# Two graph layers on one core: the stretch between the layers and the opening of layer 1 rearranged

## What is computed

```python
h = jnp.maximum(_layernorm(x, axis=-1), 0.0)
x = x + _L0_gnn_ref(h, edge_index, L0_gnn_W, L0_gnn_b)      # h@W, normed by degree, summed over edges, + b; h + gelu(..)
h = jnp.maximum(_layernorm(x, axis=-1), 0.0)
# layer 1:
message_in = jnp.concatenate((source_x, target_x, edge_x), axis=1)
message_x = _mlp(message_in, msg_W1, msg_b1, msg_W2, msg_b2)
agg = jax.ops.segment_sum(message_x, targets, num_segments=num_nodes)
update_in = jnp.concatenate((agg, node_x), axis=1)
x = x + _mlp(update_in, upd_W1, upd_b1, upd_W2, upd_b2)
```

## Time and profile before

| | us |
|---|---|
| median of 3 runs | 2396.71 (2395.64 to 2399.2) |
| the profiled execution | 2395.71, its span 2393.9, mean TensorE clock 0.938 |
| busy: TensorE, its weight loads | 2169.2, 1951.6 |
| busy: VectorE, ScalarE, GpSimd | 1706.6, 1143.6, 1600.1 |
| layer 0's edges | about 197 to 804 us of the span |
| between the layers | about 804 to 889 |
| message passes of layer 1 | about 889 to 2354 |
| tail | about 2354 to 2393.9 |

### The profile page before, as it was taken

One profiled execution on the slowest core, in us unless ns is written; L12 is line 12 of the kernel. 1 busy time (PEld: TensorE's weight loads), 2 busy tenths in 40 slices (PEclk: granted clock), 3 DMA queues, 4 the chain that ended last, 5 costly groups with the idle time before them and its releaser, 6 DMA issues.

```text
span 2393.9 us, 72611 instructions
## 1 busy us (share of the span) xinstructions
PE 2169.2 (91%) x23690; PEld 1951.6 (82%) x23690; DVE 1706.6 (71%) x4619; ACT 1143.6 (48%) x2411; POOL 1600.1 (67%) x1574
## 2 busy tenths in 40 slices
PE   2255999999999569999999999999999999999998
PEld 1143888887888458999999999999999999999995
DVE  8866888887888766666666666666666666666662
ACT  0004888888888433444444444444444444444442
POOL 5375777777775115777777777777777777777771
PEclk7566999999999758999999999999999999999999
DMA  2002111111111022333333333333333333333332
GB/s 73 1 1 44 26 27 28 27 28 28 27 27 19 4 68 59 74 73 73 76 75 74 73 73 73 73 73 76 74 74 74 75 73 75 76 74 73 73 74 36
DMA packets 345718, 133.10 MB, mean 56 GB/s; under 512 B 304301, under 2 KB 321555, under 8 KB 345587
## 3 DMA queue, kind: packets, MB, share of 16 engines
q1 hardware_dynamic: 297780, 82.40, 15.2%
q0 software_dynamic: 47808, 49.05, 11.3%
HBM read 123.78 MB, written 7.52 MB: 55 GB/s over the span
## 4 chain that ended last, share of the span: by engine, by line
PE 87%; DVE 7%; issue 3%; POOL 2%; DMA 1%; ACT 1%; SPq 0%; DVEq 0%; PEld 0%; PEldq 0%; POOLq 0%; ACTq 0%
PE psum L1737 17%; PE psum L1679 14%; PE psum L1548 12%; PE psum L1751 12%; PE psum L1580 9%; PE psum L1670 8%; PE psum L1689 5%; PE psum L1569 2%; PE psum L1715 2%; POOL rows L665 1%; PE psum L1704 1%; PE psum L1559 1%; PE psum L1640 1%; PE psum L1515 1%; DVE work L813 1%
## 5 line engine op out<-in xcount | busy, mean ns | idle before, releaser
L665 POOL DMA_INDIRECT rows<-a_rows,idx x1078 | 1049.8, 974 | 449.9 <-issue 306.0
L1319 ACT ACTIVATE hT<-psum 128x392 bf16<-128x392 f32 x1152 | 510.7, 501 | 101.6 <-PE psum L1580 93.4
L665 POOL DMA_INDIRECT rows<-g_rows,idx x416 | 431.4, 1037 | 145.8 <-issue 126.7
L1548 PE MATMUL psum<-work,hT 128*128 128x192 bf16 x3528 | 455.5, 247 | 0.3 <-ACT hT L1319 0.3
L1737 PE MATMUL psum<-edge_index,H 128*128 128x192 bf16 x4802 | 429.9, 247 | 2.4 <-DVE H L1092 2.4
L1372 ACT ACTIVATE eoT<-psum 128x512 f32<-128x512 f32 x392 | 213.8, 602 | 409.3 <-PE psum L1670 409.3
L1737 PEld LDWEIGHTS psum<-edge_index,H 128*128 128x128 bf16 x4802 | 398.9, 99 | 4.0 <-DVE H L1092 2.5
L1548 PEld LDWEIGHTS psum<-work,hT 128*128 128x128 bf16 x3528 | 324.0, 99 | 71.0 <-issue 1.4
L1580 PE MATMUL psum<-Z,one_lo 128*128 128x392 f16 x1152 | 365.5, 339 | 15.6 <-DVE Z L929 15.4
L1679 PE MATMUL psum<-wb,eoT 128*128 128x64 f32 x3136 | 376.0, 273 | 0.0
L1679 PEld LDWEIGHTS psum<-wb,eoT 128*128 128x128 f32 x3136 | 367.3, 193 | 0.1
(11 more groups left out here) (272 smaller groups left out, 2060.2 us busy)
## 6 DMA issues: line engine op xcount, KB each, us to landing
work<-in_edge_attr_dram SPq DMA_DIRECT2D x390, 128.0 KB
rows<-a_rows,idx POOLq DMA_INDIRECT x1078
Z<-slot_code SPq DMA_DIRECT2D x98, 160.0 KB
rows<-g_rows,idx POOLq DMA_INDIRECT x416
idx<-src_by_tile SPq DMA_DIRECT2D x199, 4.0 KB
wb<-b_rows SPq DMA_DIRECT2D x196, 16.0 KB, 2.0
g_rows<-Y SPq DMA_DIRECT2D x1, 1600.0 KB, 8.9
a_rows<-Y SPq DMA_DIRECT2D x6, 256.0 KB, 2.6
```

What stands on the lines that cost most here:

```text
L665: pool.indirect_dma_start(out=rows[:, k, t, :], out_offset=None, in_=table, in_offset=bass.IndirectOffsetOnAxis(ap=idx[:, k, t:t + 1], axis=0)
L1319: nc.scalar.activation(counts[:, j % 2, :, t * SLOTS:(t + 1) * SLOTS], psum[:, t % 4, 0:KEYS].rearrange("p (h m) -> p h m", m=SLOTS), ACT.Copy
L1548: ins = TT.matmul(psum[:, 4 + (j + 1) % 2, 0:NPART * D], counts[:, (j + 1) % 2, h, :], gtab[:, h, :, :].rearrange("p k d -> p (k d)"), sta ...
```

## The change

1. `centre`: the multiplication into `mean` goes; one scalar_tensor_tensor computes `Y = s1 * (-1/D) + X`.
2. The addition of `b_upd2` leaves GpSimd; VectorE does it after the message passes, ahead of the outputs. `s_xb` goes.
3. The setup between the layers goes. For the first pass `rel` is the one of layer 0 plus `pe_far`, added behind the last variance; `rnd_no`, `slot_cmp` and `pe_slot` are set by GpSimd before layer 0. (If layer 0 needed several passes, VectorE resets `rel` behind them.)
4. The opening of layer 1 on every engine: packing and spreading first, transposes of superblock 0 under them, picks, and only then the transposes of superblock 1 and the edge terms of superblock 0. TensorE's wait for `s_tab3` stands behind the packing.
5. SyncE: the features and indices of superblock 0 are loaded already during the interlude; in the loop they are loaded at the end of the turn before. Indices are issued ahead of the window load. The wait for `a_rows` is gone from SyncE; VectorE waits only for the first `C_USED` (4) chunks of it, since the passes overwrite only that part of `Y`; GpSimd waits for all. The load of the counts into `hT` moves from between the layers to the end of the passes.

```diff
+        C_USED = -(-(o + BINS * NPART * D // 2) // (T * D))
@@ SyncE
-            sp.wait_ge(s_hrow, 1)
-            sp.dma_start(hT[0:1, :], cnt_dram...).then_inc(s_cntr, 16)
...
-            def load_superblock(r, s, k, tiles, rest):
-                sp.wait_ge(summed[1], r * NSB + s + 1)
+            def load_inputs(s, k, tiles=T, rest=None):
                 if rest is None:
...
+                if k != KPE:
+                    sp.dma_start(idx[:, k, :], src_dram[:, bass.ds(s * T, T)]).then_inc(idx_in[1][k], 16)
+            def inputs_free(n, k):
+                sp.wait_ge(summed[1], n + 1)
+                if k != KPE:
+                    sp.wait_ge(added, n + 1)
+            def load_window(s, k):
                 b0 = sp.value_load(base_i[0:1, bass.ds(s, 1)], min_val=0, max_val=NP - W)
                 sp.dma_start(wb[D:2 * D, k, :], b_dram[bass.ds(b0, W), :]).then_inc(b_in[k], 16)
-                if k != KPE:
-                    sp.wait_ge(added, r * NSB + s + 1)
-                    sp.dma_start(idx[:, k, :], ...).then_inc(idx_in[1][k], 16)
+            def load_superblock(r, s, k, tiles, rest):
+                if k:
+                    inputs_free(r * NSB + s, k)
+                    load_inputs(s, k, tiles, rest)
+                load_window(s, k)
+            sp.wait_ge(s_stT, 1)
+            load_inputs(0, 0)
             for c in range(NCHUNK):
...
-            sp.wait_ge(s_ad, 16 * NCHUNK)
             sp.wait_ge(s_bd, 16 * NCHUNK)
...
+                sp.wait_ge(from_slot_ready, 2 * r * NIT + 1)
                 load_codes(r, 0, 0)
...
+                    inputs_free(r * NSB + (i + 1) * U, 0)
+                    load_inputs((i + 1) * U, 0)
...
+                inputs_free((r + 1) * NSB, 0)
+                load_inputs(0, 0)
+            sp.wait_ge(s_hrow, 1)
+            sp.dma_start(hT[0:1, :], cnt_dram...).then_inc(s_cntr, 16)
@@ GpSimd
+            nc.gpsimd.memset(rnd_no[:, :], 0.0)
+            nc.gpsimd.iota(slot_cmp[:, :], [[P, BINS]], base=-CENTRE, channel_multiplier=1, ...)
+            G.tensor_copy(pe_slot, rank32)
-            pool.wait_ge(s_var[1], NCHUNK)
-            nc.gpsimd.tensor_tensor(X[:, :, :], X[:, :, :], bu3, ALU.add).then_inc(s_xb, 1)
-            pool.wait_ge(s_ad, 16 * NCHUNK)
+            pool.wait_ge(s_ad[0], 16 * C_USED)
+            pool.wait_ge(s_ad[1], 16 * (NCHUNK - C_USED))
@@ VectorE
-                    dve.wait_ge(counts_reset[1], r + 1)
-                    dve.sem_inc(s_turn[2], 1)
-                    for k in range(3):
-                        onehots_of(0, k)
                     edges_to_slots(0, 0, first=True)
                     copy_packed(0, 0)
+                    onehots_of(0, 0)
                     edges_to_slots(0, 1, first=True)
                     picks(0, 0)
                     copy_packed(0, 1)
+                    for k in range(1, 3):
+                        onehots_of(0, k)
+                    dve.wait_ge(s_bd, 16 * NCHUNK)
                     slots_to_edges(0, 0)
...
-                link(V.tensor_scalar(mean[:, cols], s1[:, cols], 1.0 / D, None, ALU.mult))
-                V.tensor_tensor(Y[:, cols, :], X[:, cols, :], per_node(mean, c), ALU.subtract).then_inc(s_centred, 1)
+                V.scalar_tensor_tensor(Y[:, cols, :], per_node(s1, c), -1.0 / D, X[:, cols, :], ALU.mult, ALU.add
+                                       ).then_inc(s_centred, 1)
...
+            V.tensor_tensor(rel_pe, rel_pe, pe_far.rearrange(...), ALU.add).then_inc(s_pass[1], 1)
             dve.wait_ge(s_std[1], 1)
...
-            link(V.tensor_scalar(rnd_no[:, :], crowded[:, :], -1.0, None, ALU.mult))
-            message_pass_setup(link)
-            dve.wait_ge(s_pass[1], 1)
...
-            dve.wait_ge(s_ad, 16 * NCHUNK)
-            dve.wait_ge(s_bd, 16 * NCHUNK)
+            dve.wait_ge(s_pass[1], 1)
+            dve.wait_ge(s_ad[0], 16 * C_USED)
             message_passes()
-            dve.wait_ge(s_xb, 1)
+            link(V.tensor_tensor(X[:, :, :], X[:, :, :], wide(b_upd2...), ALU.add))
@@ ScalarE
+                copy_slot_src(0, 0)
                 copy_transposed(0, 0, False)
+                for u in range(4):
+                    copy_picked(0, 0, u)
                 copy_transposed(0, 1, False)
-                for g in range(2):
-                    copy_slot_src(0, g)
-                    for u in range(4):
-                        copy_picked(0, g, u)
+                copy_slot_src(0, 1)
+                for u in range(4):
+                    copy_picked(0, 1, u)
@@ TensorE
-            pe.wait_ge(s_tab3, NCHUNK)
...
+                pack_slots(0, 0)
+                spread_slot_src(0, 0)
                 transpose_edges(0, 0, True)
+                pack_slots(0, 1)
+                pe.wait_ge(s_tab3, NCHUNK)
+                for u in range(4):
+                    pick_rows(0, 0, u)
                 transpose_edges(0, 1, False)
                 edge_and_target_terms(0, 0)
-                pack_slots(0, 0)
-                spread_slot_src(0, 0)
-                pack_slots(0, 1)
-                for u in range(4):
-                    pick_rows(0, 0, u)
                 spread_slot_src(0, 1)
                 return_rows(0, 0)
```

More of the change, by code:

```diff
@@ L354, in gnn_two_layers @@
         s_tab3 = sem("s_tab3")
-        s_xb = sem("s_xb")
         s_split_v = sem("s_split_v")
@@ L489, in _ @@
             sp.dma_start(code_dram[(NCODE - 1) * P:NPT, :], code_rows[0:NPT - (NCODE - 1) * P, NCODE - 1, :]).then_inc(s_coded, 16)
-            for c in range(NCHUNK):
-                m = min(T, NB - c * T)
-                for table, held, copied, stored in ((a_dram, Y, s_ac, s_ad), (b_dram, Z, s_bc, s_bd)):
-                    sp.wait_ge(copied, c + 1)
-                    sp.dma_start(table[c * T * P:(c * T + m) * P, :].rearrange("(b p) d -> p b d", p=P),
-                                 held[:, c * T:c * T + m, :]).then_inc(stored, 16)
-            sp.wait_ge(s_ad, 16 * NCHUNK)
-            sp.wait_ge(s_bd, 16 * NCHUNK)
-            sp.wait_ge(s_coded, 32)
-            sp.wait_ge(s_mode1, 1)
-            passes1 = sp.value_load(passes1_i[0:1, 0:1], min_val=1, max_val=PASSES * ROUNDS)
             def load_codes(r, i, g):
@@ L1183, in _ @@
                 all_gathered_passes()
+                V.memset(base_pass[:, :], 0.0)
+                V.memset(base_i[:, :], 0)
+                V.tensor_copy(rel[:, :, :], dst3).then_inc(s_pdone[2], 1)
+                dve.wait_ge(s_pdone[2], passes * 4 + 1)
+                dve.sem_inc(s_turn[2], 1)
             V.memset(s1[:, :], 0.0).then_inc(s_stc, 1)
@@ L1222, in _ @@
                     variance(c - 2)
+            rel_pe = rel[:, :, :].rearrange("p (i u) t -> p i (u t)", u=U)[:, :, PE0:PE0 + PT]
+            V.tensor_tensor(rel_pe, rel_pe, pe_far.rearrange("p (i t) -> p i t", t=PT), ALU.add).then_inc(s_pass[1], 1)
             dve.wait_ge(s_std[1], 1)
@@ L1270, in _ @@
             dve.wait_ge(s_acc1, 1)
-            dve.wait_ge(s_ad, 16 * NCHUNK)
-            dve.wait_ge(s_bd, 16 * NCHUNK)
+            dve.wait_ge(s_pass[1], 1)
+            dve.wait_ge(s_ad[0], 16 * C_USED)
             message_passes()
-            dve.wait_ge(s_xb, 1)
+            link(V.tensor_tensor(X[:, :, :], X[:, :, :], wide(b_upd2[:, :].rearrange("p (b d) -> p b d", b=1), 1, NB), ALU.add))
             for c in range(0, NB, T):
```

22 lines of the change are left out of this document (15 added, 7 removed).

## The result

The changed kernel took 2361.32 us (median of 4 runs, 2359.18 to 2362.57) against 2396.36 us (2395.64 to 2399.2, 4 runs) for the kernel before: a ratio of 0.9851 with a 95% interval of 0.9834 to 0.9868. The profiled execution took 2359.18 us, its span is 2357.4 us.

The account below looks back on a forecast made before the run. TensorE at 2.4 GHz was taken to bound the passes, so gains lay outside them: 6.67 + 5.12 + 9.2 + 1.2 - 0.53 = 21.7 us off the profiled 2395.7 us, 2374.0; as a median 2375 us, range 2369 to 2382.

Parts of the forecast that it names:

- the first three parts: Centring, bias and setup between the layers: together they let TensorE start the tables 11.79 us earlier.
- the 35 us that follow: TensorE's table work between the layers, assumed to stay at 1.2 GHz and only shift earlier, with no gain of its own.
- Centring, 6.67 us: Between the layers: seven small `mean` instructions leave VectorE's unbroken chain, two of them long beside GpSimd memsets; 6.67 us saved.
- Bias, 5.12 us: Without GpSimd's add the first normalisation ends 5.12 us earlier; the add hides on VectorE in the tail.
- Setup, 0: Some 24 small VectorE instructions between the layers lie under TensorE's unbroken work, so removing them gains 0.
- the rival with the stall: The new centring form waits beside GpSimd's memset, giving back up to 5.3 us: 2380 us; chance 0.06.
- The cast ahead of layer 0, 0.53 us: One more GpSimd cast before layer 0 delays the `acc` memset and VectorE's chain; costs 0.53 us.
- Opening, 9.2 us: Layer 1's start: packing and picks no longer wait for edge features; net 9.2 us saved, bounds 5.6 and 10.
- a late clock: In layer 1's opening TensorE's clock rises late, so 5.6 us is gained instead of 9.2: 2379 us; chance 0.10.
- an opening held back: An overlooked semaphore holds layer 1's packing until the edges' old time: 2384 us; chance 0.05.
- Index order, 1.2 us: Tail: earlier index loads bring the last gathers forward, saving 1.2 us, bounds 0 and 1.3.
- The lasting low clock: TensorE stays at 1.2 GHz into layer 1's passes: 2402 us; chance 0.04, shared with something unseen in the loop.

Follow-up runs that it names:

- a_again: The changed kernel itself, run again beside the kernel before; 2361.8 us.
- a_oldopen: Changed kernel with the old order of layer 1's opening on TensorE, ScalarE and VectorE, SyncE keeping the new order; 2369.6 us.
- b_fold_t: Kernel before with only the mean folded into the centring; 2377.3 us in the lower group, 2390.5 us in the upper.
- a_biasback: Changed kernel with the bias add back on GpSimd behind the last variance; 2368.6 us in the lower group.
- b_bias_t: Kernel before with only the bias add moved from GpSimd to VectorE ahead of the outputs; 6.1 us shorter in the lower group, 4.4 in the upper.
- a_delay8_t: Changed kernel with 8 extra normalising instructions ahead of the first that counts, some 5.7 us of delay; no overall time given.
- a_delay16_t: Changed kernel with 16 extra normalising instructions ahead of the first that counts, about 11.6 us of delay; 2386.4 us.
- b_mid: Kernel before with 9 extra f32 matmuls in the middle of TensorE's idle time ahead of the tables; no overall time given.
- b_warm: Kernel before with 32 extra f32 matmuls on TensorE right ahead of the first transposes of `H`; 2384.4 us.
- the last two kernels: Changed kernel with 2 and with 19 extra normalising instructions; 3762.4 and 3776.5 us, against 3830.5 for the kernel before beside them; inconclusive.
- a_warm2: Changed kernel with extra f32 matmuls in TensorE's idle time, 9 ahead of the tables and 20 behind them; 2355.98 us.

## Why the prediction was wrong, step by step

**The step that failed** is the sentence behind the first three parts: "the 35 us that follow are its own work at the same clock; they shift whole". I had taken the clock of a stretch from one execution as a property of the kernel. It is a property of the execution: of 66 runs of the kernel before, 21 were in the lower group, and the 3 that I was shown, like the fourth of the result, were all in the upper one. At 45 of 66 that happens to four runs about one time in five. What the runs showed in place of my sentence is a stretch 14.55 us shorter, with the same TensorE instructions in it; compared within the lower group the change gains 20.4 us, near the 21.7 of the sum. The other parts of the sum were sound, and only this one put the time outside the range. The frequency by kernel, with TensorE's idle time ahead of the first transposes of `H` in the profiled execution:

| kernel | idle us | runs in the lower group |
|---|---|---|
| changed (`a_again` and the first 4) | 21.86 | 10 of 10 |
| `a_oldopen` | 21.86 | 6 of 6 |
| `b_fold_t` | 26.99 | 5 of 10 |
| `a_biasback` | 27.35 | 5 of 7 |
| `b_bias_t` | 27.64 | 9 of 10 |
| `a_delay8_t` | 27.68 | 6 of 8 |
| before | 32.75 | 21 of 66 (two of the others 7 us above it) |
| `a_delay16_t` | 33.48 | 2 of 12 |
| `b_mid` | 21.67, behind a burst | 5 of 12 |
| `b_warm` | matmuls right ahead | 9 of 10 (the tenth 5 us above) |

Shown: the 14.5 us are the clock (`b_warm` changes nothing else); starting the tables 11 us sooner makes the rise the rule instead of the exception (the delays take it back with nothing else altered); neither GpSimd's add nor the new opening is needed for that; the length of idling right ahead doesn't decide it. Not shown: what does. One regularity of the traces bears on it. In the eight traces of kernels near 2400 us in which the clock rose in the tables without extra matmuls right ahead, it rose 3.1 to 4.8 us after the first transpose (840.24 for 837.15, 848.12 for 843.32), which is within the first 16 transposes or up to 1.2 us behind them. In the two in which it had not by then, the kernel before and `b_mid`, it did not in the remaining 30 us of busy TensorE either. That reads like a single chance, but two traces don't show it, and the two runs between the groups (2390.2 and 2392.4 us, no trace kept) may be later rises. That the frequency goes up and down with the shift was the theory of the last two kernels, and is untested.

The rest, in the order of the prediction:

- **Centring, 6.67 us: right.** Measured 6.65 on VectorE's chain (807.67 to 842.61 before, 808.02 to 836.31 after), and by the parts alone 7.2 and 8.2. The new form does not stall beside a memset: the rival with the stall is out. The rule of the Trainium skill ("SBUF — State Buffer", "Who interferes with whom") fits both sides here: two SBUF inputs beside a memset, 0.69 us; the same form beside GpSimd's tensor_tensor, 5.81 us.
- **Bias, 5.12 us: right**, 5.96 to 0.84 us, and 5.1 when put back. In the tail it is hidden: the add of 3.49 us runs at 2326.12 us, the first output instruction follows it at 2329.64 us.
- **Setup, 0: right.** The `rel` add ends inside VectorE's wait for the square root. Nor is the removed setup in the 14.55 us: `b_fold_t` still has it, and its stretch from the first transpose to the entry takes 871.13 - 844.20 = 26.93 us, 1.0 more than the changed kernel's 25.97, of which some 0.7 is its clock's rise 1.5 us later (4.6 us behind the first transpose). The cast ahead of layer 0, 0.53 us: 0.76 us at the last block of layer 0 (798.76 to 799.52 us), but only 0.35 us where VectorE begins on the sums.
- **Opening, 9.2 us: right**, 9.15. My reading of the clock there was off: a mean of 0.59 in the window 911 to 912 puts the rise at 911.8 us, 4.8 us into the picks, not at 911.4. After the change it came 5.1 us into them (874.4 us), still before the pair that follows. The first picks came 32.1 us after the first transpose, not 46.6: the difference is the tables' again. The rivals with a late clock and with an opening held back are out.
- **Index order, 1.2 us: mis-sized, about 0.3 to 0.5 in this execution.** The index load was issued 1.2 us earlier in the turn (1381.0 us behind the block of 891.21, 1382.3 behind the one of 926.33 before), but the group of gathers that waits for it starts at the same place: 1385.6 us behind the block in both, with a wait of 1.91 instead of 2.12 us. I had put the wait down to the load's issue; it is its landing. The packet records of the two traces show why that did not move: of the load's 128 packets 120 had started by 2274.0 us, and the last eight at 2274.91, just as a packet of 16 KB of an instruction queue (2273.70 us, 1.22 us long) ended. In four more traces of kernels with the new order (`a_again`, `a_biasback`, `a_delay8_t`, `a_delay16_t`) the last eight start within 0.02 us of the end of such a packet; in `a_oldopen` they are late without one. In `a_warm2` no such packet falls there, the gathers wait 0.88 us, and the last sum comes 1.1 us earlier than in `a_again` (1425.41 and 1426.51 us behind the block). So most of the 1.2 us is there in an execution where nothing holds the load up; that the packet is what holds it is read from these traces and not tested. Off the path the new order did more: over 1370 us of the passes (930 to 2300 us before, 895 to 2265 after) GpSimd's waits for indices fell from 93.3 us in 71 waits to 11.8 us in 7. The gather that waits on the path, in GpSimd's timeline of the kernel after, then of `a_warm2`:

```profile
2276.78 0.94 POOL L684 DMA_INDIRECT rows<-a_rows,idx  x1 [1.91 <-DMA idx<-src_by_tile]
2275.10 0.94 POOL L684 DMA_INDIRECT rows<-a_rows,idx  x1 [0.88 <-DMA idx<-src_by_tile]
```

- **Tail: 0 counted, 0.9 gained**, since the clock rose 1.8 us earlier in it (3.8 instead of 5.7 us behind the last sum); with a clock that differs from execution to execution I can't claim this for the change.
- **The lasting low clock**, my rival on the slow side, had the right mechanism with the wrong sign: I asked whether work would lose the high clock, never whether the 35 us at the low one could win it. The row was in view, and half of 35 us is the largest single amount in the interlude. It belonged among the rivals with 17 us and a chance.
- **The rule of the Trainium skill that I quoted for this**, "TensorE: Matmul & The Clock Gate", Part 4, that transposes do not count as busy, is not borne out: in the changed kernel the clock rose at 840.24 us while TensorE had done nothing but f32 transposes since 837.15. Here the measurement decides.

## What to carry to other kernels

When TensorE works for tens of microseconds at 1.2 GHz behind an idle stretch, put half of that time into the sum as a rival, and take more than one execution before treating the clock as given: two groups of times, 14 us apart here, are its sign. Compare a change within the group, and price it there; then ask separately whether it moves the frequency. Idle time right ahead of such a stretch can be filled with a few matmuls without use (2361.8 to 2356.0 us here), but count their records and let them end before the real work is ready.

## What the runs showed of the hardware

- A program on one core had two times that repeat, 2383 and 2398 us, that differ by one rise of TensorE's clock in 35 us of f32 transposes and 64-row products; in the kernel before, 20 of 20 us busy did not bring it.
- The clock stays up for a few us without work: it fell at 860.7 us (a mean of 0.68 in the window 860 to 862), 3.3 us after the last table product ended (857.4). In `b_mid` the burst of 4.18 us raised it just as the burst ended (827.5 us), and it was at 2.4 GHz while TensorE idled (1.00 of the window 828 to 830).
- Useless f32 matmuls of 128x128 cost 0.24 us each at 2.4 GHz (`a_warm2`: 4.73 us for 20) and 0.46 us at 1.2 GHz (`b_mid`: 4.18 us for 9), two records each. A f32 transpose of the same size is one record and 0.14 us (1.09 for 8) or 0.25 us (1.97 for 8).
- The load of the indices, 4 KB in 128 packets, was issued 1.2 us earlier in its turn and in the changed kernel did not land earlier: its last eight packets started as a 16 KB packet of another queue ended (2274.91 and 2274.92 us). In `a_warm2`, without such a packet there, the gathers behind it waited 0.88 instead of 1.81 us (`a_again`).
